# Last attention of a four-layer kernel: the work of two query tiles spread evenly over both, the first head's maximum in two parts, and the reciprocals turned by matmuls

## The reference, cut to what matters

```
def _L3_xattn_ref(x, latents, mask, g_x, b_x, g_l, b_l, Wq, Wkv, Wout, g_o, b_o):
    ...
    q = jnp.einsum('bnd,de->bne', ln, Wq)
    kv_in = jnp.concatenate([xn, ln], axis=1)
    kv = jnp.einsum('bnd,de->bne', kv_in, Wkv)
    ...
    sim = jnp.einsum('bhid,bhjd->bhij', q, k)
    full_mask = jnp.concatenate([mask, jnp.ones((b, m), dtype=bool)], axis=1)
    sim = jnp.where(full_mask[:, None, None, :], sim, max_neg)
    attn = jax.nn.softmax(sim, axis=-1)
    out = jnp.einsum('bhij,bhjd->bhid', attn, v)
    ...
    out = jnp.einsum('bne,ed->bnd', out, Wout)
    return layer_norm(out, g_o, b_o)
```

## Time and profile before

| what | value |
|---|---|
| time, median of 3 runs | 2177.15 us (2177.0 to 2179.2) |
| time of the profiled execution | 2167.44 us |
| its span, first to last instruction | 2165.5 us |
| mean granted TensorE clock | 0.956 of full |
| TensorE busy | 1934.3 us, 89% |
| VectorE busy | 1487.1 us, 69% |
| ScalarE busy | 975.6 us, 45% |
| GpSimd busy | 754.9 us, 35% |
| start of unit 0, start of unit 127 | 1096.4 and 2036.3 us into the span |

### The profile page before, as it was taken

One profiled execution on the slowest core, in us unless ns is written; L12 is line 12 of the kernel. 1 busy time (PEld: TensorE's weight loads), 2 busy tenths in 40 slices (PEclk: granted clock), 3 DMA queues, 4 the chain that ended last, 5 costly groups with the idle time before them and its releaser, 6 DMA issues.

```text
span 2165.5 us, 32060 instructions
## 1 busy us (share of the span) xinstructions
PE 1934.3 (89%) x11157; PEld 1304.9 (60%) x11157; DVE 1487.1 (69%) x2740; ACT 975.6 (45%) x2083; POOL 754.9 (35%) x1146
## 2 busy tenths in 40 slices
PE   6996999679999979979689999999989999998899
PEld 3883899434799958855545445545654555554544
DVE  5764111484344467968769998989778999988655
ACT  5662343333111431258744555545445555544445
POOL 1002011002322100000057666766546777766400
PEclk9997999889999999989899999999999999998999
DMA  3603899204599730020023333333222333332201
GB/s 111 201 1 119 275 324 330 85 0 158 182 322 323 251 111 1 1 83 1 1 49 75 78 76 75 77 73 78 58 51 72 78 78 77 79 72 71 53 1 39
DMA packets 191180, 226.79 MB, mean 105 GB/s; under 512 B 28939, under 2 KB 167085, under 8 KB 191021
## 3 DMA queue, kind: packets, MB, share of 16 engines
q1 hardware_dynamic: 183725, 201.98, 31.8%
q0 software_dynamic: 7296, 22.78, 3.1%
HBM read 127.64 MB, written 29.91 MB: 73 GB/s over the span
## 4 chain that ended last, share of the span: by engine, by line
PE 38%; DVE 11%; ACT 6%; issue 1%; ACTq 0%; DVEq 0%
PE ps L640 35%; ACT w_odd L1787 4%; DVE small L2519 4%; DVE small L2521 3%; DVE small L2522 1%; PE ps L1205 1%; PE ps L1213 1%; PE ps L1106 1%; ACT L1787 0%; DVE x_res L2485 0%; DVE small L2400 0%; PE ps L1206 0%; PE ps L1115 0%; DVE arena L2473 0%; DVE w_odd L2530 0%
## 5 line engine op out<-in xcount | busy, mean ns | idle before, releaser
L1898 POOL COPY arena<-w_odd 32x512 f32<-32x512 f32 x1024 | 625.5, 611 | 326.3 <-DVE w_odd L2530 274.0
L640 PE MATMUL ps<-arena,w_odd 128*128 128x128 f32 (+4 forms) x2352 | 449.2, 450 | 3.0 <-DVE arena L2192 1.2
L640 PE MATMUL ps<-arena 128*64 128x256 f32 (+4 forms) x3248 | 394.2, 372 | 8.6 <-DVE arena L2323 4.8
L1787 ACT ACTIVATE w_odd<-ps,small 128x1101 f32<-128x1101 f32 x256 | 301.8, 1179 | 95.3 <-DVE small L2519 53.1
L2530 DVE STREAM_TRANSPOSE w_odd<-w_odd 128x1024 f32<-128x1024 f32 x256 | 317.5, 1243 | 26.3 <-ACT w_odd L1787 17.8
L640 PEld LDWEIGHTS ps<-arena 128*64 128x64 f32 (+4 forms) x3248 | 259.3, 155 | 121.8 <-issue 24.7
L640 PEld LDWEIGHTS ps<-arena,w_odd 128*128 128x128 f32 (+3 forms) x2352 | 249.1, 190 | 108.8 <-issue 103.5
L2519 DVE TENSOR_REDUCE small<-ps 128x1 f32<-128x1101 f32 x128 | 166.8, 1303 | 65.8 <-PE ps L640 65.8
L1772 ACT ACTIVATE arena<-ps 77x256 f32<-77x256 f32 x128 | 48.7, 380 | 334.1 <-PE ps L1206 334.1
L1882 POOL DMA_INDIRECT token_rows<-arena x62 | 60.0, 968 | 292.4 <-DVE arena L2213 292.4
L2521 DVE TENSOR_REDUCE small<-ps 128x1 f32<-128x1024 f32 x128 | 155.5, 1215 | 0.0
(11 more groups left out here) (398 smaller groups left out, 3025.8 us busy)
## 6 DMA issues: line engine op xcount, KB each, us to landing
arena<-w_odd SPq DMA_DIRECT2D x1024, 64.0 KB
w_odd<-in_s_w SPq DMA_DIRECT2D x32, 1024.0 KB, 7.2
w_odd<-in_s_wgu SPq DMA_DIRECT2D x30, 704.0 KB, 5.8
w_even<-in_s_w SPq DMA_DIRECT2D x15, 1024.0 KB, 7.1
arena<-expert_rows_in SPq DMA_DIRECT2D x62, 130.0 KB, 4.5
w_odd<-in_s_wd SPq DMA_DIRECT2D x30, 256.0 KB, 3.6
out_feat<-in_s_wgu SPq DMA_DIRECT2D x10, 704.0 KB, 5.8
expert_rows_in<-zero_row POOLq DMA_DIRECT2D x1, 5070.0 KB, 32.0
```

What stands on the lines that cost most here:

```text
L640: return pe.matmul(o, lhsT, rhs, start=start, stop=stop, **kw)
L1787: act.activation(s6_p[u % 2][h], s6_sc[h], ACT.Exp, bias=s6_nm[:, u % 2, h:h + 1], accum_out=s6_sm[:, g % 2, 2 * (u % 2) + h:2 * (u % 2) + ...
L1898: pool.tensor_copy(s6_d[u % 4][32 * j:32 * j + 32, :, 256 * i:256 * i + 256], s6_pm[u % 2][32 * i:32 * i + 32, :, 256 * j:256 * j + 256]). ...
```

## The change

It changes stage 6 in five ways.

1. One piece is computed in every unit, where an even unit had two.
2. `weigh(g)` is cut in two: tiles 0 to 3 of the keys in the odd unit 2g + 3, tiles 4 to 8 in the even unit 2g + 4. The multiplication with `s6_r` moves from the start of that even unit to the start of the next odd one; `project`, `normed` and `added` move by one unit too, and the loop is one unit longer.
3. `scores` signals once more, when the first 512 columns of both heads are written. VectorE takes head 0's maximum over those 512 during the rest of the scores, then over the other 589, and joins the two parts with a `tensor_tensor` as head 1 has it.
4. The reciprocals are taken at the end of the odd unit whose sums they are, behind the transposes, no longer at the start of the odd unit after.
5. The tile `s6_rb` and VectorE's copy to it are gone. `sums_turn` makes the broadcast itself: four matmuls whose stationary operand is a column of reciprocals read 64 times over, with the identity as the moving one.

```diff
@@ scores
                     for i in range(2):
                         for h in range(2):
                             r = 64 * h
                             last = mm(PS[:, 3 * h + i, :], s6_q[n % 2][r:r + 64, q0:q0 + P], s6_k[n % 2][r:r + 64, i * 512:(i + 1) * 512])
-                    last.then_inc(a6_s, 1)
+                        last.then_inc(a6_s, 1)
@@ sums_turn
                     for i in range(2):
-                        last = pe.transpose(PS[:, bank, i * P:(i + 1) * P], s6_rb[g % 2][:, 2 * i:2 * i + 2].rearrange("p h d -> p (h d)"), ident[:, :])
+                        for h in range(2):
+                            r = 64 * h
+                            last = mm(PS[r:r + 64, bank, i * P:(i + 1) * P], s6_rc[:, g % 2, 2 * i + h:2 * i + h + 1].broadcast_to([P, DH]), ident[:, :])
                     last.then_inc(r6_mm, 1)
@@ TensorE's loop
-                    if even and n < 16:
-                        for i in (j, j + 1):
-                            piece(n, i, free_bank(("w", n, i))).then_inc(r6_mm, 1)
                     if not even and 3 <= u < NU + 3:
                         sums_turn((u - 3) // 2)
-                        weigh((u - 3) // 2)
-                    if even and u >= 4 and (u // 2 - 2) % 32 >= 28:
-                        project(u // 2 - 2)
+                    if even and 4 <= u < NU + 4:
+                        weigh((u - 4) // 2, 4, NKT)
+                    if n < 16:
+                        piece(n, j, free_bank(("w", n, j))).then_inc(r6_mm, 1)
+                    if not even and 3 <= u < NU + 3:
+                        weigh((u - 3) // 2, 0, 4)
+                    if not even and u >= 5 and ((u - 5) // 2) % 32 >= 28:
+                        project((u - 5) // 2)
@@ VectorE's loop
-                    if not even and 3 <= u < NU + 3:
-                        g = (u - 3) // 2
-                        dve.wait_ge(a6_p, 4 * g + 4)
-                        link(dve.reciprocal(s6_rc[:, g % 2], s6_sm[:, g % 2]))
-                        if g >= 2:
-                            dve.wait_ge(r6_mm, r6_no["r", g - 2] + 1)
-                        dve.tensor_copy(s6_rb[g % 2], s6_rc[:, g % 2].unsqueeze(2).broadcast_to([P, 4, DH])).then_inc(a6_rb, 1)
...
-                        dve.wait_ge(a6_s, 2 * u + 2)
-                        dve.tensor_reduce(s6_nm[:, u % 2, 0:1], s6_sc[0], AX.X, ALU.max, negate=True).then_inc(a6_mx, 1)
-                        m = s6_nm[:, u % 2, 1:2]
-                        link(dve.tensor_reduce(m, s6_main, AX.X, ALU.max, negate=True))
-                        dve.tensor_tensor(m, m, s6_cm[:, u % 2, 1:2], ALU.min).then_inc(a6_mx, 1)
+                        dve.wait_ge(a6_s, 3 * u + 2)
+                        dve.tensor_reduce(s6_cm[:, u % 2, 0:1], psf[:, 0:512], AX.X, ALU.max, negate=True)
+                        dve.wait_ge(a6_s, 3 * u + 3)
+                        for h in range(2):
+                            m = s6_nm[:, u % 2, h:h + 1]
+                            link(dve.tensor_reduce(m, s6_rest[h], AX.X, ALU.max, negate=True))
+                            dve.tensor_tensor(m, m, s6_cm[:, u % 2, h:h + 1], ALU.min).then_inc(a6_mx, 1)
...
                         for h in range(2):
                             dve.wait_ge(a6_p, 2 * u + h + 1)
                             dve.transpose(s6_pm[u % 2][:, h], s6_pm[u % 2][:, h]).then_inc(t6_done, 1)
+                        if not even:
+                            g = u // 2
+                            if g >= 2:
+                                dve.wait_ge(r6_mm, r6_at["r", g - 2])
+                            dve.reciprocal(s6_rc[:, g % 2], s6_sm[:, g % 2]).then_inc(a6_rb, 1)
```

More of the change, by code:

```diff
@@ L380, in build @@
         N7 = {77 + 4 * t: t for t in range(8)}
-        r6_no, r6_sb, done = {}, {}, {"act": 0, "dve": 0}
-        for u in range(NU + 5):
+        r6_no, r6_at, r6_sb, done = {}, {}, {}, {"act": 0, "dve": 0}
+        for u in range(NU + 6):
             even = u % 2 == 0
@@ L422, in turned @@
             if u >= 4:
[L423 removed]
+                eng.wait_ge(r6_mm, r6_at["v", (u - 4) // 2])
         STEPS = 6
@@ L2497, in stage6 @@
                     piece(0, j, j).then_inc(c6_sb, 1)
-                for u in range(NU + 6):
+                for u in range(NU + 7):
                     even = u % 2 == 0
-                    if even and 4 <= u < NU + 4:
-                        g = (u - 4) // 2
+                    if not even and 5 <= u < NU + 5:
+                        g = (u - 5) // 2
                         c = (g // 4) % 8
```

77 lines of the change are left out of this document (44 added, 33 removed).

## The result

The change makes the kernel slower. Its median is 2222.82 us in four runs (2221.11 to 2226.49), beside 2178.18 (2177.0 to 2183.54) for the kernel before: a ratio of 1.0202, interval 1.018 to 1.0224. The prediction had 2157.6 and a range of 2141 to 2176.

A forecast was written before the change was run, and what follows sets the result against it. TensorE was taken to bound odd units and the loop of the scores even ones. Steady units -17.5, units beside the rows -3, clock -4, projections and stage end +5 made -19.5 us: 2157.6 from 2177.15, range 2141 to 2176.

The forecast's parts named there:

- What bounds the kernel: Steady units of stage 6 before the change: TensorE ends odd units at 7.00 us, the scores' loop even ones at 6.86.
- The loop of the scores: From a unit's first scores matmul through maxima, joins and exponentials to the next scores: 6.63 us, under the 6.86 before.
- TensorE's share: TensorE's work per unit: even 6.76, 6.34, 6.82, 6.37 us; odd 6.91, 6.91, 6.06, 6.06 us.
- the wait for the last keys: Before a head pair's first scores, ScalarE copies the last piece behind the exponentials: 0.27 us on top, once in eight units.
- The sum: All terms for the whole kernel: -17.5 - 3 - 4 + 5 = -19.5 us, giving 2157.6.
- the clock: Two or three falls of the clock behind TensorE's idle time in steady units gone: 4 us off, bounds 0 and 10.
- The 3 off in the 32 units beside the rows: Units beside the rows for stage 7, whose odd units carry another turn of 0.3: 3 us off.
- the 8 on for projections: Projecting units, three of the first batch and one of the second, where `ctx_turn` waits 2.0 us: 8 us on.
- `ctx_turn` of a projecting unit waits for the multiplication: In projecting units VectorE has `added` ahead of the multiplication, so `ctx_turn`, due at 2.4 us, waits 2.0.
- What was forecast for projections proper: In four projecting units `ctx_turn` waits 2.0 us for the multiplication: 8 us on.
- The rival on the slower side: Head 1's join asks 0.15 us too late, the next GpSimd copy goes first: loop 7.3, time 2202 us; chance 0.13.
- The side on which the time fell: The whole kernel gets slower, beyond the 0.2% that a measurement can tell from no change: chance 0.14.

The follow-up runs named there:

- 4: The kernel before with only head 0's maximum split in two parts: 2134.8 us, ratio 0.9849.
- 14: The kernel before with head 1's join as a one-operand `tensor_reduce` over two neighbouring columns: 2144.51 us, ratio 0.9905.
- 16: The kernel before with head 0's maximum split and both joins as `tensor_reduce`: 2129.99 us, ratio 0.9832.
- 7: The changed kernel with row turns and projections ahead of `weigh`, multiplication ahead of `added`, sums' rows by VectorE's copy and two transposes: 2120.76 us, ratio 0.9801.
- 5: The kernel before with only the sums turned by four broadcast matmuls, without VectorE's copy: 2160.97 us, ratio 0.9985.
- 1: The changed kernel with row turns for stage 7 ahead of `weigh`'s first part: 2175.6 us, ratio 1.0037 to the kernel before.
- 2: The changed kernel with row turns and projections ahead of `weigh`'s first part: 2145.83 us, ratio 0.9897 to the kernel before.

## Why the prediction was wrong

**What bounds the kernel: right.** Odd units were TensorE's and even ones the loop's. Shortening the loop alone (4, 14, 16) shortens even units alone, and taking work from TensorE (7) shortens odd ones.

**The loop of the scores: right in kind.** Forecast were 6.63 and less for units that start late; 6.46 to 6.61 came. Joins were forecast at 0.5 to 0.6 and 0.15; here they took 0.32 and 0.17, in the mean 0.285. That the joins wait for the ends of GpSimd's copies is shown by 14 and by the trace of before.

**TensorE's share: 0.1 short in each unit that it binds.** Its units were 6.76, 6.91, 6.91, 6.82 in the forecast and 6.85, 7.02, 7.07, 6.95 in the trace. `sums_turn` was put at 0.25 more than the transposes. In front of `weigh` that was right: 0.21 on the unit (5). In front of a piece, where it stands now, the step from `ctx_turn` to the piece grew by 0.46 and the piece by 0.10 (7): the change from half of the array's columns to all of them was priced too low. With the wait for the last keys, 0.58 for 0.27, eight units gained 1.13 and not 1.85.

**The sum.** Forecast were 17.5 off for steady units and 4 for the clock. Stretches 4 to 60, 70 to 76 and 108 to 124 gave 23.6 off. That this is near is luck: at 1.13 per eight, 78 steady units give 11.0, and the other 12.6 are the clock, above the forecast's bound of 10. Units 31, 47, 75, 111, 119, 121 and 123 of the kernel before ran partly at the lower clock (0.68 to 0.81 over the unit) and took 8.60 to 10.58, together 14.6 above the 7.01 of their like. In the changed kernel all seven are at 1.00, and of the excess 1.9 are left, in unit 111. The 3 off in the 32 units beside the rows became 32.9 on, and the 8 on for projections became 30.7 on, with 5.2 more at the end.

**The step that failed is the place of `weigh` in the three-bank rotation.** I wrote that in the changed order "`ctx_turn` of a projecting unit waits for the multiplication", and took the row turns as "another turn of 0.3". I had found the one turn that is three places behind `weigh` in a steady unit, and used it everywhere. It holds for the second batch's projections (2.15 in unit 127). Where a row turn or a projection of the first batch stands behind `weigh`, that turn is the piece of the even unit, and `ctx_turn` of the projecting unit is the third behind `project`. Its wait isn't for an instruction in front of the transposes but behind them, so the unit contains its own loop and then the piece: 10 us instead of 6.5. Experiments 1 and 2 only move turns within odd units and take 34.2 off beside the rows, 24.8 at the first batch's projections and 7.4 at the second's, 66.4 in all. Of the first, 38% was the lower clock behind the idle time, which the forecast had only counted as a gain.

**What was forecast for projections proper was right**, in a kernel in which the failed step was mended: the wait was 2.14 for 2.0, and taking it away gave 8.8 in units 60 to 70 for 8.

**The rival on the slower side** (head 1's join misses its copy's end) did not come about: the join takes 0.17. The side on which the time fell had 0.14, and none of that for the rotation.

**What a reader could have found beforehand**: the order of the turns was there in full. Going through it once for every kind of unit, and asking of each turn which one is three places ahead and when that one is copied out, gives the loss with the numbers of the earlier trace rows. Head 1's exponential ends 6.7 into an even unit (1316.18 + 1.18 - 1310.64), 6.3 in one that starts late by 0.4. Behind it come the second transpose, 1.25, the multiplication, 0.4, and a piece, 1.3 to 1.7: 9.3 to 9.7 at full clock, some 3 more than 6.5, and this in eight units beside the rows and four at the projections of the first batch.

Open: why TensorE waited in an earlier stage of this one profile, which makes the 12 us by which the starts of stage 6 differ.

## What to carry to other kernels

When work is moved in a rotation of few buffers, walk through the rotation for each kind of iteration, the rare ones first. The turn that needs the buffer changes as soon as one more stands in between, and it must never need what the same iteration produces last.

Give added work to an engine that does not end the iteration, and price a wait together with the clock that it costs. A small instruction in the chain of a loop is worth a look at its operands: here 0.16 us of work cost 0.54, and one operand fewer was worth 1% in the kernel before, 0.6% and less in the others.

## What the runs showed of the hardware

- A `tensor_tensor` on two 128x1 columns takes 0.16 us alone and up to 0.61 while GpSimd copies 32x512 tiles, and ends with the copy that it falls into; a `tensor_reduce` over 128x2 takes 0.155 in both cases.
- Two transposes of 128x128 on TensorE show 0.38 us, and four matmuls that make the same tile from broadcast columns, in pairs side by side, 0.66; full-array work behind them takes 0.10 longer.
- The clock can fall behind idle times of TensorE and comes back only later, but not every such time brings a fall. Of the eight waits of 2.72 to 3.06 in units 78 to 106 seven did and one of 2.72 (unit 82) did not; of the four of 7.55 in units 62 to 68 all did. In the first case the granted clock of the 32 units was 0.94, and 1347 records were busy 13.1 us more than 1346 at 1.00.
